# Gated attention with its decays made by bf16 products of rows, and TensorE making a slot's scores before the transposes of the tile behind

## The reference

```
log_D = cum[s] - cum[t] + ig[t]          for t <= s, else -inf
D     = exp(log_D - max_t log_D)
C     = (q k^T / 4) * D
Cn    = C / (max(|sum C|, exp(-max)) + 1e-6)
h     = Cn v;  per head (h - mean) * rsqrt(var + 1e-6) * ln_scale;  x = x + h
```

## Time and profile before

| | us |
|---|---|
| median of 3 runs | 2200.45 |
| lowest, highest | 2195.76, 2201.08 |
| profiled execution, its own time | 2195.36 |
| its span in the trace | 2193.7 |
| mean granted clock of TensorE in it | 0.834 of full speed |
| busy: PE, PEld | 1514.8 (69%), 938.5 (43%) |
| busy: DVE, ACT, POOL | 1441.1 (66%), 1114.8 (51%), 570.7 (26%) |

### The profile page before, as it was taken

How to read it: one execution, slowest core, us unless ns; L and a number is a source line. 1 busy time by engine, 2 the same in 40 slices (tenths; PEclk the granted TensorE clock), 3 DMA queues, 4 the chain that set the end, 5 groups by cost and what they waited for, 6 DMA issues and landing times. The chain is left out here.

```text
span 2193.7 us, 34574 instructions
## 1 busy us (share of the span) xinstructions
PE 1514.8 (69%) x11413; PEld 938.5 (43%) x11458; DVE 1441.1 (66%) x2920; ACT 1114.8 (51%) x1540; POOL 570.7 (26%) x910
## 2 busy tenths in 40 slices
PE   3349999999399758787754575559999954776111
PEld 3326555555277634444421233335555542444000
DVE  6648888886245337667765999825555556775796
ACT  4517777777112124343444788723333334777454
POOL 3412333333200132322231344200010001111663
PEclk9999999999599969888985566569999977788555
DMA  5643555554200032112101000011010120000211
GB/s 168 196 108 86 136 131 131 134 131 95 80 1 0 4 75 48 43 45 62 34 7 60 0 1 1 1 39 35 25 34 23 27 82 20 1 1 1 48 48 39
DMA packets 94834, 120.62 MB, mean 55 GB/s; under 512 B 26128, under 2 KB 78552, under 8 KB 90108
## 3 DMA queue, kind: packets, MB, share of 16 engines
q1 hardware_dynamic: 94716, 119.12, 21.2%
HBM read 79.30 MB, written 22.09 MB: 46 GB/s over the span
## 5 line engine op out<-in xcount | busy, mean ns | idle before, releaser
L610 DVE TENSOR_REDUCE ratt_nmax<-ratt_psS 128x2 f32<-128x512 f32 x512 | 318.2, 683 | 92.9 <-PE ratt_psS L502 92.5
L576 ACT ACTIVATE ratt_E<-ratt_psT 128x1024 f32<-128x1024 f32 x256 | 255.0, 1023 | 106.0 <-PE ratt_psT L524 106.0
L502 PE MATMUL ratt_psS<-ratt_K,ratt_Q 72*128 72x256 bf16 x1024 | 204.3, 284 | 39.0 <-DMA ratt_K<-context_parts 33.6
L524 PE MATMUL ratt_psT<-ratt_Q,ratt_K 75*128 75x256 bf16 x1024 | 195.9, 275 | 5.5 <-DMA ratt_Q<-ratt_rows 5.2
L537 PE MATMUL ratt_psO<-ratt_E,ratt_V 128*32 128x256 f32 x2048 | 137.9, 387 | 0.7 <-ACT ratt_E L576 0.7
L502 PEld LDWEIGHTS ratt_psS<-ratt_K,ratt_Q 72*128 72x128 bf16 x1024 | 79.9, 99 | 135.1 <-issue 64.8
L524 PEld LDWEIGHTS ratt_psT<-ratt_Q,ratt_K 75*128 75x128 bf16 x1024 | 99.5, 98 | 23.5 <-DMA ratt_Q<-ratt_rows 5.6
L1355 PE MATMUL gatt_psA<-gatt_DA,gatt_same 128*128 128x512 f32 x128 | 89.3, 787 | 28.9 <-DVE gatt_DB L1240 25.3
L1174 POOL TENSOR_TENSOR gatt_DA<-gatt_own,gatt_a 128x1024 f32<-128x1024 f32 x32 | 61.6, 1937 | 143.8 <-PE gatt_psA L1358 90.6
L3302 PE MATMUL final_psT<-final_identh,final_Z 128*128 128x128 f16 x64 | 8.3, 310 | 110.4 <-ACT final_Z L3336 110.4
L1238 DVE TENSOR_REDUCE gatt_mx<-gatt_psA 128x16 f32<-128x1024 f32 x32 | 39.0, 1219 | 65.4 <-PE gatt_psA L1358 64.7
(11 more groups left out here) (461 smaller groups left out, 4000.3 us busy)
## 6 DMA issues: line engine op xcount, KB each, us to landing
ratt_Q<-z_parts SPq DMA_DIRECT2D x32, 576.0 KB
ratt_K<-context_parts SPq DMA_DIRECT2D x96, 192.0 KB
gatt_V<-in_ctx_dram SPq DMA_DIRECT2D x16, 512.0 KB, 6.2
z_parts<-prep_ZS SPq DMA_DIRECT2D x48, 128.0 KB, 2.7
context_parts<-prep_CS SPq DMA_DIRECT2D x48, 128.0 KB, 2.3
head_sums<-ratt_O SPq DMA_DIRECT2D x64, 72.0 KB
all_X<-in_x_dram SPq DMA_DIRECT2D x8, 512.0 KB
prep_C<-in_ctx_dram SPq DMA_DIRECT2D x8, 512.0 KB
```

Source lines behind the costliest of these rows:

```text
L502: mm = nc.tensor.matmul(psS[:, RING[h], c * D:(c + 1) * D], Q9[0:R, buf, h, k % 2, c * P:(c + 1) * P], K9[0:R, buf, h, k % 2, :], start=Tr ...
L524: mm = nc.tensor.matmul(psT[:, p % 2, e, c, :], K9[0:RM, buf, h, u, c * P:(c + 1) * P], Q9[0:RM, buf, h, u, :], start=True, stop=True)
L576: nc.scalar.activation(E[:, 2 * b + p // 2, 2 * (p % 2):2 * (p % 2) + 2], psT[:, p % 2], ACT.Exp, scale=SCALE).then_inc(exped, 1)
L610: nc.vector.tensor_reduce(nmax[:, k % 2, h, :], psS[:, RING[h]].rearrange("p (c t) -> p c t", c=2), AX.X, ALU.max, negate=True).then_inc(m ...
```

## The change

The decay of a tile is now one product of two bf16 matrices of 94 rows. R holds, on its rows, the constant diagonal of the mask, the constant choice of a head, and a itself; LT holds the mask, minus the running maximum, and ones. a and the maximum are each split into three bf16 parts. For this, a is transposed once for a group (turn_a), its running maximum is taken by two scans on VectorE (running_maximum), the maximum is transposed back (turn_maximum, take_maximum), GpSimd makes the parts (split_rows), and SyncE writes them to a buffer in DRAM and reads them back into LT and R (decay_rows). psA then holds the difference already, and ScalarE takes its exp straight into PB, where weigh multiplies in place. The inverse root of the variance is one power on GpSimd (power) over 64 columns in place of the logarithm, exp and the four small steps.

The order is one slot for a tile, T + 12 slots in all, written out without a loop: in slot n TensorE makes the decay of tile n-6, the scores of tile n-7, the transposes and the values of tile n-8; the front of group n // 4 and the tail of group n // 4 - 3 lie in the slots by n % 4. The queries have three buffers; the context is read from CT in place, without the copy CG; sq is Z's memory; constants for R and LT are copied once.

Of the functions not shown here, front_gates, front_logs and front_sums are the three parts of the old front; tail_centre is the old part 0 of tail and runs at n % 4 = 0; tail_variance is the old part 1, nine steps, at n % 4 = 1; weigh is the old one without the second buffer.

```diff
-        self.QT = s.sb("QT", [P, 2, KC, G * P])
+        self.QT = s.sb("QT", [P, queries, KC, G * P])
...
+    MX_ROW, A_ROW, ROWS = L, L + 3 * HC, L + 3 * HC + 6
...
+                def decay_rows(g):
+                    w = g % 2
+                    sp.wait_ge(split, g + 1)
+                    if g > 1:
+                        sp.wait_ge(rows_in[w], (g // 2) * ROWS_IN)
+                    sp.dma_start(rows_dram[w].rearrange("n p h t -> h n p t"), parts[:]).then_inc(rows_out, 16)
+                    sp.wait_ge(rows_out, g * 16 + 16)
+                    if g > 1:
+                        sp.wait_ge(decayed, (g - 1) * G)
+                    for p in range(3):
+                        sp.dma_start(LT[MX_ROW + p * HC:MX_ROW + (p + 1) * HC, w].rearrange(
+                            "h j c u t -> h (j c) (u t)"), rows_dram[w, 1, p].rearrange(
+                                "(x h) t -> h x t", h=HC)).then_inc(rows_in[w], 16)
+                    for u in range(2):
+                        for_u = rows_dram[w, 0].rearrange("p h (u t) -> u p h t", u=2)[u]
+                        sp.dma_start(R[A_ROW + 3 * u:A_ROW + 3 * u + 3, w].rearrange("p j c h t -> p (j c h) t"),
+                                     for_u).then_inc(rows_in[w], 16)
+                def keys(g, half):
+                    after = g * G - 2 + 2 * half
+                    if after > 0:
+                        sp.wait_ge(heads.scored, after)
+                    for c in range(KC):
+                        for h in range(HC):
+                            rows = slice(h * DH, (h + 1) * DH)
+                            first = g * (G * P) + half * HG
+                            sp.dma_start(KX[rows, half, c, h, :], CT[rows, c, first:first + HG]).then_inc(
+                                heads.kx_in[half], 16)
+                rows_of_context(0)
+                keys(0, 0)
+                keys(0, 1)
+                for g in range(NG):
+                    decay_rows(g)
+                    if g > 0:
+                        keys(g, 0)
+                        sp.wait_ge(v_copied, g * 2 + 2)
+                        rows_of_context(g + 1)
+                    if g > 0:
+                        keys(g, 1)
...
+                def split_rows(g):
+                    step = Steps(pool, split_steps, 4, g)
+                    x = pair[:, 0:2]
+                    pool.wait_ge(pair_steps, g * PPER + PPER)
+                    if g > 0:
+                        pool.wait_ge(rows_out, g * 16)
+                    step(gp.tensor_copy(parts[:, :, 0], x))
+                    step(gp.tensor_tensor(rest[:, 0], x, parts[:, :, 0], ALU.subtract))
+                    step(gp.tensor_copy(parts[:, :, 1], rest[:, 0]))
+                    step(gp.tensor_tensor(rest[:, 1], rest[:, 0], parts[:, :, 1], ALU.subtract))
+                    step.end()
+                    gp.tensor_copy(parts[:, :, 2], rest[:, 1]).then_inc(split, 1)
+                def power(g):
+                    pool.wait_ge(t_steps, g * TPER + 13)
+                    gp.tensor_tensor(tw[:, 9].rearrange("p j h -> p (j h)"), tw[:, 8].rearrange("p j h -> p (j h)"),
+                                     half[:], ALU.pow).then_inc(powered, 1)
...
+                norm.on_pool(pool, 0)
+                pool.wait_ge(w_in, 144)
+                for g in range(NG + 3):
                     if is_group(g + 1):
                         norm.on_pool(pool, g + 1)
+                    if is_group(g - 3):
+                        power(g - 3)
                     if is_group(g):
+                        split_rows(g)
+                    if is_group(g - 3):
+                        add(g - 3)
...
+                def running_maximum(g):
+                    step = Steps(dve, pair_steps, PPER, g)
+                    dve.wait_ge(a_turned, g + 1)
+                    if g > 0:
+                        dve.wait_ge(split, g)
+                        dve.wait_ge(m_turned, g)
+                    step(v.tensor_copy(pair[:, 0], psG[0:GH, 0:P]))
+                    for u in range(2):
+                        x = pair[:, 0, u * L:(u + 1) * L]
+                        step(v.tensor_tensor_scan(pair[:, 2, u * L:(u + 1) * L], x, x, LOW, ALU.max, ALU.max))
+                    step(v.tensor_scalar(pair[:, 1], pair[:, 2], -1.0, None, ALU.mult))
+                    step.end()
+                def take_maximum(g):
+                    dve.wait_ge(m_turned, g + 1)
+                    v.tensor_copy(mx[:, g % 3].rearrange("p j h -> p (j h)"), psG[:, 0:GH]).then_inc(m_taken, 1)
...
+                def tail_scale(g):
+                    step = Steps(dve, t_steps, TPER, g)
+                    step.n = 13
+                    dve.wait_ge(powered, g + 1)
+                    step(v.tensor_tensor(tw[:, 10], tw[:, 9], tw[:, 7], ALU.mult))
+                    step(v.tensor_tensor(cen[:, g % 2], cen[:, g % 2], spread(tw[:, 10], 3, DH), ALU.mult))
+                    step.end()
+                norm.on_vector(dve, 0, Z)
                 v.memset(KX[:, 1], 0.0).then_inc(kx_set, 1)
                 dve.wait_ge(w_in, 144)
                 v.tensor_tensor(WC[:], WK_[:], WV_[:], ALU.add).then_inc(wc_steps, 1)
                 dve.wait_ge(ready, READY)
+                v.tensor_copy(R[:].rearrange("p w j c h t -> p (w j c) (h t)"),
+                              spread(rbase[:].rearrange("p h t -> p (h t)"), 1, 2 * G * KC)).then_inc(const_set, 1)
+                v.tensor_copy(LT[:].rearrange("p w j c u t -> p (w j c) (u t)"),
+                              spread(lbase[:].rearrange("p u t -> p (u t)"), 1, 2 * G * KC)).then_inc(const_set, 1)
+                for n in range(SLOTS):
+                    g, i = at(n)
+                    if i == 0:
+                        if is_group(g):
+                            front_gates(g)
+                        if is_tile(n - 7):
+                            weigh(n - 7)
+                        if is_group(g - 3):
+                            tail_centre(g - 3)
                     if i == 1:
+                        if is_group(g):
+                            front_logs(g)
+                        if is_tile(n - 7):
+                            weigh(n - 7)
+                        if is_group(g + 1):
+                            norm.take_stats(dve, g + 1)
+                        if is_group(g):
+                            front_sums(g)
+                        if is_group(g - 3):
+                            tail_variance(g - 3)
+                    if i == 2:
+                        if is_group(g):
+                            running_maximum(g)
+                        if is_tile(n - 7):
+                            weigh(n - 7)
+                        if is_group(g + 1):
+                            if is_group(g):
+                                dve.wait_ge(z_turned, g * KC + KC)
+                            norm.normalise(dve, g + 1, Z)
+                        if is_group(g - 3):
+                            tail_scale(g - 3)
                     if i == 3:
+                        if is_group(g):
+                            take_maximum(g)
+                        if is_tile(n - 7):
+                            weigh(n - 7)
...
+                def turn_z(g, k):
+                    if k == 0:
+                        pe.wait_ge(norm.normed, g * G + G)
+                        if g > 0:
+                            pe.wait_ge(m_taken, g)
+                    else:
+                        pe.wait_ge(q_taken, g * KC + k)
...
+                def turn_a(g):
+                    pe.wait_ge(f_steps, g * FPER + FPER)
+                    nc.tensor.transpose(psG[0:GH, 0:P], a[:].rearrange("p j h -> p (j h)"), ident[:]).then_inc(
+                        a_turned, 1)
+                def turn_maximum(g):
+                    pe.wait_ge(pair_steps, g * PPER + PPER - 1)
+                    nc.tensor.transpose(psG[:, 0:GH], pair[:, 2], ident[0:GH, 0:GH]).then_inc(m_turned, 1)
+                def decay(t):
+                    g, j = at(t)
+                    w = g % 2
+                    if j == 0:
+                        pe.wait_ge(rows_in[w], (g // 2 + 1) * ROWS_IN)
+                    if t == 0:
+                        pe.wait_ge(const_set, 2)
+                    if t > 0:
+                        pe.wait_ge(d_done, t)
+                    for c in range(KC):
+                        mm = nc.tensor.matmul(psA[:, c, :], LT[0:ROWS, w, j, c].rearrange("p u t -> p (u t)"),
+                                              R[0:ROWS, w, j, c].rearrange("p h t -> p (h t)"), start=True, stop=True)
+                    mm.then_inc(decayed, 1)
+                turn_z(0, 0)
+                turn_z(0, 1)
+                gates_of(0)
+                for n in range(SLOTS):
+                    g, i = at(n)
+                    t = n - 6
+                    if is_group(g) and i == 1:
+                        running_sums(g)
+                    if is_tile(t):
+                        decay(t)
```

(54 more changed lines are left out.)

391 lines of the change are left out of this document (127 added, 264 removed).

## The result

The changed kernel took 2226.36 us, median of 4 runs (2221.91 to 2232.27), against 2198.52 for the kernel before beside it (2195.76 to 2201.08): ratio 1.0132, 95% interval 1.0115 to 1.0150, 28 us slower. The forecast had the side right and said 2258, 60 us slower, so more than half of the predicted loss did not come. The two profiled executions are 33.8 us apart (2229.14 and 2195.36), more than the medians, because single executions of a kernel scatter by 5 to 10 us. The profiled execution has a span of 2227.4 us and a mean granted clock of 0.815 (before 0.834).

A forecast was written before the change was run, and what follows sets the result against it. Neither TensorE nor VectorE is full: the 44.3 us period is a chain through both. With X = 13.2, P = 40.3 + X = 53.5 and end 877 + 6P + X = 1211, 62 us later: 2195.4 + 62 = 2258 us, range 2168 to 2275.

The forecast's parts named there:

- The power stands in the sum in full: Slot 2 of each period: GpSimd's whole power adds to the chain, not only its excess over four steps beside it.
- likeliest case: The dear power, 8 to 14 us, with or without scans held up: chance 0.52, 2222 to 2270; own range 2225 to 2285.
- X: GpSimd's power of 64 columns in slot 2: 13.2 us taken if paid by column, 1.1 if mostly fixed start.
- the formula: End of the gated attention = 877 + 6P + X, period P = 40.3 + X; 1211 us with X = 13.2.
- T = 0 of the first period: Start of the first period's turn_z(g+1, 0), after constants, keys and decay rows: near 819 us.
- The first period without a tail: First period, without variance 3.6, power and scale 1.5: 35.2 us, next T at 854.
- Slot 2: Period's part with power, VectorE's scans, weigh, normalise, split_rows, tail_scale and take_maximum: X + 6.1 us.
- rival D: Scans not held up, only the power's excess over weigh and normalise counts: 4 us a period less, 2232; no separate chance.
- The break-even of X = 4.2: Length of GpSimd's power, 4.2 us, at which the change neither gains nor loses time.
- A: Cheap power on GpSimd, X up to 3: 2174 us at 1.1, 2187 at 3, faster by up to 1.2%; chance 0.26.
- B: Power on GpSimd between, X of 3 to 8: 2187 to 2222 us, 7 us per us of X; chance 0.17.
- C: TensorE's clock holds through idle 3 to 4 us: about 6 us a period less, 2222 with dear power; chance 0.05.

The follow-up runs named there:

- e1: Changed kernel with GpSimd raising only 32 of the 64 columns to the power, the rest set to 1.0 (wrong output): 2187.70 us, ratio to before 0.9956.
- e2: Changed kernel with tail_scale moved from slot 2 to the end of slot 3, and split_rows ahead of the power: 2190.48 us, ratio to before 0.9969.
- e3: Changed kernel with the power replaced by the old Ln, Exp and four refining VectorE steps: 2187.35 us, ratio to before 0.9951.
- e5: Changed kernel with 20 unread products added on TensorE ahead of turn_z(g+1, 0), groups 4 to 7, in the long idle time: 2223.17 us, ratio 1.0102.
- e6: Changed kernel with 4 unread products added on TensorE ahead of turn_z(g+1, 1), groups 4 to 7, in the short idle time: 2207.61 us, ratio 1.0047.
- run 8: Not a label: the words are "a run 8 us slower than before", the formula's result at X = 5.43; no kernel has this name.
- e4: Changed kernel with each slot's transposes of the tile behind put ahead of its scores on TensorE: 2210.55 us, ratio to before 1.0076.
- e10: e7 with tail_scale moved one slot further, into slot 0 of the next group behind gates and weights: 2196.40 us, ratio to before 0.9989.
- e7: Changed kernel with the edits of e2 and e4 together: 2177.64 us, ratio to before 0.9915.
- e12: Changed kernel with edits of e2, e3 and e4, plus KX cleared first and first rstd ahead of GpSimd's constants: 2153.95 us, ratio to before 0.9803.

## Why the prediction was right in direction and wrong in size

**That it gets slower, and by which mechanism: shown.** "The power stands in the sum in full": e1 changes nothing but the power and moves the run by 7.6 us per us (7 predicted), e2 moves the wait (and split_rows with it), e3 takes it away; each brings 36 to 39 us. The named sign, TensorE idle over 10 us ahead of turn_z(g+1, 0) with take_maximum as what ended it, is there. The periods are 51.2 us, not 53. The time of 2226.4 us lies at the very edge of the likeliest case's own range (2225 to 2285).

**X, the step that failed.** The sum's largest term was mis-sized: 13.2 us stood for the power of 64 columns, 10.55 were measured. Of the stage's miss of 27.9 us (449.9 forecast, 422.0 measured), 7 x (13.2 - 10.55) = 18.6 are this term. The upper end had each column at the rate that the earlier trace rows give for four columns less an addition's own 0.19 us. The true line has a part of about 0.4 us that is not paid by column (1.01 - 4 x 0.16). The extrapolation took only 0.19 of it off and multiplied the rest by sixteen. A price from four columns, for 64, was the wrong thing to take a point from; the middle of the ends would have been no better founded, but the likeliest case's range should have begun lower. The page GPSIMD Engine Reference of the Trainium skill, section 3.1 Elementwise, has 2.6 cycles for an element of a two-input addition. The trace agrees for additions and not for the power: its 0.16 us are an estimated 190 cycles of the 1.2 GHz with which that page reckons.

**The rest of the sum was off in both directions.** With X = 10.55 the formula gives a stage of 431.3 us; 9.3 less were measured, so even with the right X the loss of the stage would have been forecast at 44 us, for 34.5:
- T = 0 of the first period came 65.7 us into the stage, not 57.7: +8.0. First decay matmuls were forecast for 814 and are at 825.4, which is 820.8 if this stage had begun as early as the one before.
- The first period without a tail took 27.7 us, not 35.2: -7.5. It was built with the low clock, and it ran at 0.94. That is this execution: in e5's, with the same code up to there, it took 31.5 us at 0.82.
- Four full periods took 198.3 us (46.9, 49.0, 51.2, 51.2), where 4 x 50.85 = 203.4 were due: -5.1.
- From the last turn_z to the end 130.3 us instead of 134.9: -4.6.

**Two errors inside the period cancel.** Slot 2 was to take X + 6.1 us; from the end of the variance (993.19) to turn_z (1006.38) it takes 13.2, that is X + 2.6. The scans, the weights and the normalisation run under the power and are not held up: rival D's premise is right, and the step that failed here is that a scan which starts 0.3 us after the power waits for it: the scans take 282 to 283 ns. Against that, the gates take 6.8 us instead of 3.5, because behind the idle time ahead of turn_z(g+1, 1) the clock is low, which stood in no term (the 32 gate matmuls take 6.9 us, and 3.8 in e6, where that idle time is filled). From turn_z to the end of the variance it is 38.0 us and not 34.2. So D's 2232 (6 x 4 us off 2258 would be 2234) is near the measured time by luck: it has an X of 13.2 and no slow gates, and the two errors cancel.

**The break-even of X = 4.2.** By e1's slope and the two medians it lies at 10.55 - (2226.4 - 2197.4) / 7.6 = 6.7 us. At X = 5.43 the formula has a run 8 us slower than before, and e1 is 10 faster. The terms of the sum beside X were together too long by 14 us there: 395.5 us of stage for 381.1.

**The rivals.** A and B are out by the width of the power. C, "the clock holds", is out: the gates and the scores behind the long wait are at 0.50 to 0.55. Its price of 6 us a period was of the right size: e5 gets back 3 us, e6 7 and e4 7, e5 behind the long wait, e6 and e4 in the gates and the scores behind them. The keys and the decay rows held nobody up, as forecast.

## What to carry to other kernels

A slow instruction on a side engine costs what is queued behind its wait, so ask first where the wait stands, and then how long it is: moving the wait by one slot was worth as much as halving the power, and moving it one further lost half of that again to the additions that came with it. When one engine runs at two clocks, look for the short idle times that your order of instructions makes; e4 and e6 won 16 and 19 us, by two steps of each slot swapped or by useless work added. Don't extrapolate the price of an unseen operation from one small instance when the term is multiplied by the number of groups.

## What the runs showed of the hardware that was not expected

- GpSimd's power with f32 operands: 1.01 us for 4 columns, 5.43 for 32, 10.55 for 64, each on 128 partitions.
- VectorE isn't held up by a power that runs on GpSimd: scans with both operands in SBUF take 0.28 us under it, four normalisation steps 1.37. Beside GpSimd's additions, casts and memsets its steps take longer: 1.22 us becomes 3.41 beside the addition to X (e10), 1.37 becomes 2.14 beside split_rows's casts and subtractions (e7), 1.38 becomes 8.23 beside memsets (e12). The page SBUF — State Buffer of the Trainium skill, section Who interferes with whom, says that a VectorE instruction with two SBUF inputs contends with a GpSimd instruction that reads SBUF, and that the shared ports are an exclusive lock. The trace agrees for the addition in e10, and not for the power, which reads SBUF too.
- TensorE's granted clock fell to 0.50 for the 6.8 us of gates behind an idle time of 2.1 us (0.86 on average from 962.0 to 965.8 us, with the idle time's end in it), and was at 1.00 in the gates when 8 matmul records of 2.0 us in all lay in that idle time (e6).
